# Cross-attention values per tile with their sums, divided behind the product, in a decoder layer

## The chip, the cores and the metric

One core of a Trainium2 chip runs the whole kernel in one launch. The metric is the device time of one execution, in microseconds (us), as the median of several. PE is TensorE, DVE VectorE, ACT ScalarE, POOL GpSimd, SP the sync engine that only launches DMAs here.

## What is computed

A decoder layer over 2 x 1024 tokens of 256 numbers, 16 heads of 16, float32: self-attention, then cross-attention over 77 context rows with a mask, then a mixture of 8 experts with the two best for each token; after each a residual and a layer norm. The part at issue, shortened:

```python
energy = jnp.einsum('bhqd,bhkd->bhqk', Q, K) * scale
energy = jnp.where(m == 0, -1000000000.0, energy)
attn = jax.nn.softmax(energy, axis=-1)
out = jnp.einsum('bhqk,bhkd->bhqd', attn, V)
out = out.transpose(0, 2, 1, 3).reshape(B, S, HID)
return out @ Wo + bo
```

## The kernel before

The stages are self-attention (to about 490 us), cross-attention (`for n in range(NT)`, 16 tiles of 128 tokens, n = 4g+i, `TG` = 4 groups), and the experts (46 blocks of 128 sorted rows).

Cross-attention of tile n before the change:
- PE `scores2(n)` (L611): scores of 16 heads into banks 0 to 3 (`quad`, columns 0 to 307), three tiles ahead of the values (`FAR = 3`).
- DVE `take(n)`: L1062 copies them out with the mask by a minimum (`s2_taken`), L1069 takes each head's maximum. POOL `shift(n)` subtracts it, ACT `exp2(n)` is the exponential, in place in `sc2`.
- DVE `sum_probs(n)` (L1074, L1076): sums over 77 and reciprocals. POOL `divide(n)` (L1798) multiplies them in; the last two tiles' on DVE (`last_divide`, L1092).
- PE `turn_probs(n)` (L629): ten 128-wide transposes in three pieces into banks 4 and 5, each piece copied to `pT` by ACT (L1516).
- PE `values2(g, half)` (L648): once for four tiles, with the placed values `vbd` as the stationary side and 512 queries moving; the result lies turned, [channel, query], in banks 6 and 7. ACT copies it to `o2T`, `project_o2(g)` (L657) multiplies by Wo, and DVE `residual2(g)` adds it to `xres` and takes moments; POOL `root`, DVE `root_moments` and `norm_x2(g)` (L1110) end the norm.

Between these lie, once for each group: `turn_x1` (L589) and `project_q2` (L596) for the next group's queries; `turn_x2` (L669) and `logits2` (L693) for the experts' router; DVE `top_two`. ACT `keep_high` writes the bf16 high half of the rows to send, `low_x2` (L1175, DVE) the low half. When half of the tokens are ranked (`rank(0)`, `rank(1)` on PE), DVE `place(0)` (L1141 to L1161) works out their sorted rows, `rowof`; POOL `scatter` (L1785) sends 8 tiles twice with indirect DMAs, SP waits for all 16 and loads the first blocks (L425), and PE `turn_block` (L843) begins the experts.

Of the kernel before, what the change touches and what calls it, by code (L numbers as in the profile page):

```python
# [5 lines left out]
ALU = mybir.AluOpType  # L6
# [7 lines left out]
P = 128  # L14
B, S, D = 2, 1024, 256
H, HD = 16, 16
SC = 77
# [16 lines left out]
SR = 4  # L34
FAR = 3
# [4 lines left out]
PAIR_CHUNKS = [(2 * j * SC // P, ((2 * j + 2) * SC - 1) // P) for j in range(HALF // 2)]  # L40

# [19 lines left out]
MASK_STEPS = 9  # L61
SOON = 14
LATE = 6
# [13 lines left out]
def build(nc, t):  # L77

    with ExitStack() as ctx:
# [65 lines left out]
        vbd = sb("vbd", [P, B, 2, VC, P])  # L145
# [60 lines left out]
        sum2 = sb2("sum2", [P, SR, H])  # L206
        inv2 = sb2("inv2", [P, SR, H])
        pT = sb2("pT", [P, 2, VC, 512])
        o2T = sb2("o2T", [P, 2, 512])
        logits = sb2("logits", [P, NT, NE])  # L210
# [30 lines left out]
        last_shifted, last_divided = sem("last_shifted"), sem("last_divided")  # L241
# [4 lines left out]
        s2_summed, s2_recip, p2_done, p2_turned, pT_done = map(sem, ("s2_summed", "s2_recip", "p2_done", "p2_turned", "pT_done"))  # L246
        o2_ready, o2T_done = sem("o2_ready"), sem("o2T_done")
# [36 lines left out]
        SCORED = (9, 13)  # L284
        X2_BANK = (6, 6, 0)
# [32 lines left out]
        def _(sp):  # L318
# [11 lines left out]
            def load_late():  # L330

                late = [(w_in[n][:, :, :], t[n].rearrange("(c p) n -> p c n", p=P)) for n in ("cwq", "cwo")]
                late += [(before[:, :], t["before"]), (b1[:, :, :], t["b1"].rearrange("e (c p) -> p e c", p=P)),
# [56 lines left out]
            for h, s0, n, c, row in V_RUNS:  # L390
                sp.dma_start(vbd[row:row + n, :, :, c, h * HD:(h + 1) * HD].rearrange("p b h d -> p (b h) d"),
                             v2[s0:s0 + n, :, :].rearrange("p b (h d) -> p (b h) d", h=2)[:, :, h * HD:(h + 1) * HD]).then_inc(v2_placed, 16)
# [47 lines left out]
            sp.wait_ge(o2_ready, 2 * TG)  # L440
# [18 lines left out]
        def _(pe):  # L459
# [139 lines left out]
            def scores2(n, half):  # L599

                g, i = n // 4, n % 4
                if half == 0:
# [4 lines left out]
                    if n == NT - 2:  # L607
                        pe.wait_ge(ranks_taken, 1)
# [27 lines left out]
            def values2(g, half, queries=slice(0, 4 * P)):  # L636

                if half == 0:
                    pe.wait_ge(pT_done, 12 * g + 3 * (queries.stop // P))
                    pe.wait_ge(q2_done, min(2 * g + 4, 2 * TG))  # L640
                    if g:
                        pe.wait_ge(y2_done, 4 * g)
                        pe.wait_ge(x2T_done, min(2 * g, 2 * TG - 4))
# [1255 lines left out]
```

## Time and profile before

| | us |
|---|---|
| median of 3 runs | 855.1 (852.06 to 857.89) |
| the profiled execution's own time | 856.25 |
| its span, first to last instruction | 854.4 |
| DVE busy | 639.0 (75%) |
| PE busy | 713.2 (83%) |
| ACT busy | 487.8 (57%) |
| POOL busy | 305.5 (36%) |

The busy shares are means over the whole program; the change touches the stretch from about 490 to 630 us, so the rows below are read there. A timeline row is start, length, engine, line, operation, output<-inputs, shapes, count, and in brackets how long the engine had waited and for what.

### The profile page before, as it was taken

The page shows a single profiled execution, that of the slowest core. Times are in us where ns is not written, and L with a number is a line of the kernel's source. Part 1 is how long each engine was busy: PE and PEld are TensorE (multiplying, and loading weights), DVE is VectorE, ACT ScalarE, POOL GpSimd, SP SyncE. Part 2 cuts the span into 40 slices and gives each one's busy share as a digit, 9 for nine tenths or more (in the row PEclk, how much of TensorE's full clock was granted, in tenths as well). Part 3 has the DMA queues.
Part 4 walks back from the last instruction along what each step waited for, and adds up shares of the span by engine and source line. Part 5 has one row for each costly group of instructions (what it writes and reads, how often), then busy time and mean ns, then how long its engine had stood idle before and what let it go on. Part 6 is the DMA issues. An engine that isn't in the chain of part 4 may idle for free.

```text
span 854.4 us, 14878 instructions
## 1 busy us (share of the span) xinstructions
PE 713.2 (83%) x4760; PEld 332.1 (39%) x4760; DVE 639.0 (75%) x1087; ACT 487.8 (57%) x982; POOL 305.5 (36%) x249
## 2 busy tenths in 40 slices
PE   6789999999999999999998868867679888789800
PEld 3442222223222222222222235545367566667600
DVE  3487888877888888887875689999737446689765
ACT  2225677777777677776777554342436566457622
POOL 8000600000000398881002575666712554444411
PEclk9898999999999999999999888887679999899965
DMA  7746040030400689883000090000241333412121
GB/s 196 187 110 148 16 93 21 19 75 20 94 20 25 155 239 278 260 253 125 2 1 1 1 380 14 1 2 7 75 124 52 100 105 90 143 53 90 58 99 49
DMA packets 51171, 80.75 MB, mean 95 GB/s; under 512 B 16468, under 2 KB 35415, under 8 KB 49689
## 3 DMA queue, kind: packets, MB, share of 16 engines
q1 hardware_dynamic: 37065, 44.91, 19.2%
q0 software_dynamic: 9952, 31.29, 11.8%
q10 hardware_dynamic: 4080, 3.61, 1.7%
q8 instruction: 42, 0.69, 0.4%
q14 instruction: 32, 0.26, 0.1%
HBM read 48.21 MB, written 33.11 MB: 95 GB/s over the span
## 4 chain that ended last, share of the span: by engine, by line
PE 54%; DVE 26%; DMA 6%; issue 5%; ACT 4%; POOL 2%; SPq 1%; DVEq 1%; another core or an unknown queue 1%; ACTq 0%; POOLq 0%
PE bank L544 12%; PE bank L536 12%; PE quad L517 11%; DVE rowmax L959 6%; PE quad L868 6%; PE bank L885 5%; DMA kstack<-k_parts 3%; PE bank L468 2%; DVE hl L1189 2%; DVE sc L1062 2%; ACT probs L1495 2%; DVE sum L1074 2%; DVE max L1069 2%; DMA qstack<-q_parts 1%; DVE attn_all L1175 1%
## 5 line engine op out<-in xcount | busy, mean ns | idle before, releaser
L959 DVE TENSOR_REDUCE rowmax<-quad 128x1 f32<-128x1024 f32 x256 | 303.0, 1218 | 77.1 <-PE quad L517 76.5
L1495 ACT ACTIVATE probs<-bank 128x512 f32<-128x512 f32 x512 | 284.3, 595 | 115.6 <-PE bank L536 112.8
L536 PE MATMUL bank<-qstack,kstack 98*128 98x512 bf16 x512 | 195.0, 389 | 12.9 <-ACT probs L1495 11.2
L517 PE MATMUL quad<-kstack,qstack 96*128 96x512 bf16 x512 | 178.4, 388 | 15.2 <-DVE rowmax L959 6.6
L868 PE MATMUL quad<-xbT,w 128*128 128x128 bf16 x1104 | 121.1, 224 | 25.6 <-DVE hl L1189 16.0
L544 PE MATMUL bank<-probs,v_all 128*32 128x512 f32 x1024 | 140.3, 617 | 0.0
L536 PEld LDWEIGHTS bank<-qstack,kstack 98*128 98x128 bf16 x512 | 49.0, 97 | 193.9 <-ACT probs L1495 163.2
L868 PEld LDWEIGHTS quad<-xbT,w 128*128 x1104 | 91.3, 100 | 58.5 <-issue 43.3
L1619 ACT ACTIVATE hid<-quad,b 128x128 f32<-128x128 f32 x184 | 52.6, 369 | 65.1 <-PE quad L868 49.5
L517 PEld LDWEIGHTS quad<-kstack,qstack 96*128 96x128 bf16 x512 | 48.6, 99 | 77.4 <-DVE rowmax L959 39.8
L1839 POOL DMA_INDIRECT y_tokens<-ysb,dest x46 | 47.7, 1038 | 84.1 <-DVE ysb L1203 75.3
L1737 POOL DMA_DIRECT2D w1raw<-in_w x8 | 6.5, 806 | 188.1 <-PE bank L468 188.1
L885 PE MATMUL bank<-w,hh 128*128 x184 | 71.8, 392 | 1.7 <-DVE hl L1189 1.7
L1189 DVE TENSOR_TENSOR hl<-hid,hh 128x512 bf16<-128x512 f32 x46 | 42.8, 930 | 26.1 <-ACT hh L1625 23.2
L1773 POOL TENSOR_TENSOR lnv<-lnv,power 128x4 f32<-128x4 f32 (+1 forms) x14 | 19.1, 1367 | 109.4 <-DVE lnv L1014 109.0
L885 PE MATMUL bank<-w,hl 128*128 x184 | 51.3, 279 | 0.0
L1793 POOL TENSOR_TENSOR sc<-sc,max 128x1232 f32<-128x1232 f32 x15 | 34.4, 2296 | 45.0 <-DVE max L1069 45.0
L1516 ACT ACTIVATE pT<-bank 128x512 f32<-128x512 f32 (+1 forms) x48 | 23.7, 524 | 41.4 <-PE bank L629 41.1
L629 PE MATMUL bank<-ident,sc 128*128 128x128 f32 (+1 forms) x160 | 30.7, 337 | 15.7 <-POOL sc L1798 6.6
L1785 POOL DMA_INDIRECT x_sorted<-attn_all,rowof x32 | 32.8, 1024 | 17.4 <-issue 5.5
L1200 DVE TENSOR_TENSOR ysb<-bank,b 128x256 f32<-128x256 f32 x46 | 19.4, 422 | 25.5 <-PE bank L885 15.0
L1798 POOL TENSOR_TENSOR sc<-sc,inv 128x1232 f32<-128x1232 f32 x14 | 31.4, 2251 | 12.6 <-DVE inv L1076 12.6
(184 smaller groups left out, 951.3 us busy)
## 6 DMA issues: line engine op xcount, KB each, us to landing
xb<-x_sorted SPq DMA_DIRECT2D x46, 129.0 KB
x_sorted<-blank POOLq DMA_DIRECT2D x6, 774.0 KB, 9.1
w1raw<-in_w POOLq DMA_DIRECT2D x8, 512.0 KB, 6.1
w2raw<-in_w POOLq DMA_DIRECT2D x8, 512.0 KB, 6.3
w_split<-w1two POOLq DMA_DIRECT2D x8, 512.0 KB, 5.7
w_split<-w2two POOLq DMA_DIRECT2D x8, 512.0 KB, 4.4
w<-w_split SPq DMA_DIRECT2D x16, 256.0 KB, 5.2
w<-w_split SPq DMA_DIRECT2D x4, 1024.0 KB, 11.8
```

The lines of the kernel that those rows point to most:

```text
L517: mm = pe.matmul(bank[2 * (p % 2) + e], q, kstack[slot][0:MAXROW, j, e * 512:e * 512 + 512], start=True, stop=True)
L536: mm = pe.matmul(bank[4 + i % 2], kstack[slot][0:KROWS, j, kt * P:kt * P + P], qstack[slot][0:KROWS, half, j, :], start=True, stop=True)
L544: pe.matmul(bank[6][32 * j:32 * j + VW, :], v_all[:, u // 2, kt, j, :], probs[:, i % PR, :], start=(kt == 0), stop=(kt == KT - 1), skip_gr ...
L868: mm = pe.matmul(bank[m % 3][:, fc * P:(fc + 1) * P], w1[half][c][fc][:, bass.ds(at, P)], xbT[:, m % 3, 2 * part + c, :], start=(k == 0), ...
L885: mm = pe.matmul(bank[Y_BANK[m % 2]][:, 0:n], a[:, m % 2, fc, :], w2[fc][:, bass.ds(at * (2 * D // P), n)], start=(step == 0), stop=(fc == ...
L959: dve.tensor_reduce(rowmax[:, k % 2, p:p + 1], quad[:, 2 * (p % 2):2 * (p % 2) + 2, :].rearrange("p a n -> p (a n)"), AX_X, ALU.max).then_ ...
L1189: dve.tensor_tensor(hl[:, m % 2, :, :], hid[:, m % 2, :, :], hh[:, m % 2, :, :], ALU.subtract).then_inc(hl_done, 1)
L1495: act.activation(probs[:, i % PR, :], bank[4 + i % 2], ACT.Exp, scale=INV4).then_inc(probs_ready, 1)
L1619: act.activation(hid[:, m % 2, fc, :], bank[m % 3][:, fc * P:(fc + 1) * P], ACT.Relu, bias=b1[:, bass.ds(e, 1), fc]).then_inc(hid_done, 1)
L1785: pool.indirect_dma_start(xs[h], bass.IndirectOffsetOnAxis(ap=rowof[:, j, n:n + 1], axis=0), xsend[:, n, :], None).then_inc(scattered[h], 16)
L1793: pool.tensor_tensor(sc, sc, over_heads(max2[:, n % SR, :]), ALU.subtract).then_inc(s2_shifted, 1)
L1839: pool.indirect_dma_start(ys[h], bass.IndirectOffsetOnAxis(ap=dest[:, m % XB:m % XB + 1], axis=0), ysb[:, m % YB, :], None, bounds_check=2 ...
```

## The change

The division moves behind the value product. `vbd` gets a column of ones for each head (17 columns for a head, `OW`), so the product brings the sum along. `values2(n)` now runs for each tile, with `pT` stationary and `vbd` moving; the result has the queries on the partitions and goes into columns 308 to 443 of banks 0 and 1, beside the scores. DVE `scale2(n)` takes the reciprocal of the sums and multiplies, into `o2n`. `turn_o2(g)` on PE transposes four tiles to banks 6 and 7, from where it goes on as before. `sum_probs`, `divide` and `last_divide` go. All 16 `low_x2` tiles move from DVE to POOL, eight of them inside the stage. `turn_x1`, `turn_x2`, `turn_probs`, `project_o2`, `top_two`, `rank(0)`, `rank(1)` and `place(0)` get other places, and several waits are added.

```diff
-                if n < NT - 2:
-                    pe.wait_ge(p2_done, n + 1)
-                else:
-                    pe.wait_ge(last_divided, n - NT + 3)
+                pe.wait_ge(p2_exp, n + 1)
...
+                    if n > FAR:
+                        pe.wait_ge(o2_scaled, n - FAR + (1 if i == 0 else 0))
...
+            def values2(n):
+
+                i, b = n % 4, n // 4 // 2
+                pe.wait_ge(pT_done, 3 * n + 3)
+                pe.wait_ge(s2_taken, n + FAR if i == 1 else min(n + FAR + 1, NT))
+                if n:
+                    pe.wait_ge(o2_scaled, n)
+                for half in range(2):
+                    for c in range(VC):
+                        lo, hi = (0, HALF) if c == 0 else V_HEADS[c]
+                        mm = pe.matmul(O2[half][:, lo * OW:hi * OW], pT[0:VROWS[c], half, c, n % PT * P:n % PT * P + P],
+                                       vbd[0:VROWS[c], b, half, c, lo * OW:hi * OW], start=(c == 0), stop=(c == VC - 1), skip_group_check=True)
+                mm.then_inc(o2_ready, 1)
+
+            def turn_o2(g, tiles=range(4)):
...
+                for half in range(2):
+                    for i in tiles:
+                        tr = pe.transpose(bank[6 + half][:, i * P:i * P + P], o2n[:, i, half * P:half * P + P], ident[:, :])
...
+                    turn_probs(n, lambda k: None)
+                    values2(n)
+                    turn_x1(g + 1)
+                    for half in range(2):
+                        project_q2(g + 1, half)
                     for half in range(2):
                         next_scores(half)
...
+            def scale2(n):
+
+                out = quad[:, 0:2, FREE - 12:FREE - 12 + HALF * OW].rearrange("p a (h d) -> p a h d", d=OW)
+                inv = inv2[:, n % 2, :].rearrange("p (a h) -> p a h", a=2)
+                dve.wait_ge(o2_ready, n + 1)
+                dve.reciprocal(inv, out[:, :, :, HD]).then_inc(o2_recip, 1)
+                dve.wait_ge(o2_recip, n + 1)
...
+                dve.tensor_tensor(o2n[:, n % 4, :].rearrange("p (a h d) -> p a h d", a=2, d=HD), out[:, :, :, 0:HD],
+                                  inv.rearrange("p a (h o) -> p a h o", o=1).to_broadcast([P, 2, HALF, HD]), ALU.mult).then_inc(o2_scaled, 1)
...
-                if n == NT - 5:
-                    place(0)
                 if n + FAR in SCORED:
                     top_two(SCORED.index(n + FAR))
...
+                if n == NT - 4:
+                    place(0)
```

The rows of order below are the instructions of one engine in queue order, with the line numbers of their own kernel (those after the change differ). First PE around tile 5 (i = 1), before, from `turn_x1` to `turn_x2`:

```order
L589 MATMUL bank<-ident,x 128x128 x8
L629 MATMUL bank<-ident,sc 128x128 x8
L596 MATMUL bank<-x1T,cwq 128x512 x4
L629 MATMUL bank<-ident,sc 104x128 x2
L611 MATMUL quad<-kbd,q2T 128x154 x8
L669 MATMUL bank<-ident,xres 128x128 x8
```

and after, from the second half of V(5) to the scores of tile 9, L614 x8 being those of tile 8 (turned probabilities are L629, scores L614, V L646):

```order
L646 MATMUL quad<-vbd,pT 128x136
L646 MATMUL quad<-vbd,pT 128x51
L646 MATMUL quad<-vbd,pT 128x34
L646 MATMUL quad<-vbd,pT 128x51
L646 MATMUL quad<-vbd,pT 128x34
L592 MATMUL bank<-ident,x 128x128 x8
L599 MATMUL bank<-x1T,cwq 128x512 x4
L614 MATMUL quad<-kbd,q2T 128x154 x8
L629 MATMUL bank<-ident,sc 128x128 x8
L614 MATMUL quad<-kbd,q2T 128x154 x4
L629 MATMUL bank<-ident,sc 104x128 x2
L614 MATMUL quad<-kbd,q2T 128x154 x4
```

V(5) now stands ahead of `turn_x1` and of the projection; the turns of tile 5, which stood between these two, now lie ahead of V(5) (the L629 rows here are tile 6's), and the scores of tile 8 come behind all of it.

DVE, before, from the take of tile 13 to the first copy of `place(0)` (L1141):

```order
L1062 TENSOR_TENSOR sc<-quad,cap 128x1232
L1069 TENSOR_REDUCE max<-sc 128x16
L1175 TENSOR_TENSOR attn_all<-xres,attn_all 128x256 x4
L1074 TENSOR_REDUCE sum<-sc 128x16
L1076 RECIPROCAL inv<-sum 128x16
L1074 TENSOR_REDUCE sum<-sc 128x16
L1076 RECIPROCAL inv<-sum 128x16
L1141 COPY ranked<-quad 128x72
```

and after, from the last take (tile 15) on; `scale2` is L1082 and L1086, the residual L1106:

```order
L1070 TENSOR_TENSOR sc<-quad,cap 128x1232
L1075 TENSOR_REDUCE max<-sc 128x16
L1097 TENSOR_TENSOR sc<-sc,max 128x1232
L1082 RECIPROCAL inv<-quad 128x16
L1086 TENSOR_TENSOR o2n<-quad,inv 128x256
L1106 TENSOR_TENSOR xres<-bank,xres 128x256 x2
L1109 BN_STATS stats<-xres 128x6
L1106 TENSOR_TENSOR xres<-bank,xres 128x256
L1109 BN_STATS stats<-xres 128x6
L1106 TENSOR_TENSOR xres<-bank,xres 128x256
L1109 BN_STATS stats<-xres 128x6 x2
```

Seven operations of moments follow, and then `place(0)` (L1146): it now stands behind the last take, its shift, `scale2(12)` and `residual2(2)`.

POOL, before, from the first scatters on (L1793 is a shift, L1773 a root, L1839 sends an expert's output):

```order
L1798 TENSOR_TENSOR sc<-sc,inv 128x1232 x2
L1785 DMA x_sorted<-attn_all,rowof 2944x258 x2
L1793 TENSOR_TENSOR sc<-sc,max 128x1232
L1785 DMA x_sorted<-attn_all,rowof 2944x258 x2
L1773 TENSOR_TENSOR lnv<-lnv,power 128x4
L1785 DMA x_sorted<-attn_all,rowof 2944x258 x12
```

and after (L1772 shift, L1757 bias, L1778 low half, L1752 root, L1764 scatter):

```order
L1772 TENSOR_TENSOR sc<-sc,max 128x1232
L1757 TENSOR_TENSOR xres<-x,cbo_row 128x256 x2
L1772 TENSOR_TENSOR sc<-sc,max 128x1232
L1778 TENSOR_TENSOR attn_all<-xres,attn_all 128x256 x4
L1752 TENSOR_TENSOR lnv<-lnv,power 128x4
L1764 DMA x_sorted<-attn_all,rowof 2944x258 x16
L1778 TENSOR_TENSOR attn_all<-xres,attn_all 128x256 x4
L1752 TENSOR_TENSOR lnv<-lnv,power 128x4
```

All 16 scatters now stand in one piece behind the last shift and root.

## Rows read from the trace of the kernel before

**Rows 1.** Table of stretches: length; busy (count) of PE, PEld, DVE, ACT, POOL; clock; DMA.

```profile
489.50:615.50 126.00, 94.03 (x657) 61.13 (x656) 117.34 (x213) 53.74 (x90) 82.58 (x52) 0.83 0.21 78
615.50:628.10 12.60, 8.33 (x59) 5.75 (x59) 0.00 (x0) 3.06 (x6) 4.92 (x6) 0.64 0.43 131
628.10:854.40 226.30, 158.32 (x1713) 121.05 (x1713) 148.03 (x441) 116.71 (x316) 85.38 (x75) 0.88 0.27 85
```

**Rows 2.** Chain of waits of the cross stage, shares by line.

```profile
by line: DVE sc L1062 11.2%; DVE sum L1074 10.8%; DVE max L1069 9.2%; DVE attn_all L1175 7.1%; PE bank L629 7.0%; DVE xres L1110 5.1%; PE quad L611 4.3%; PE bank L693 4.2%; POOL sc L1798 3.6%; issue 3.3%; DVE x L1054 3.3%; DVE xres L1101 3.
```

**Rows 3.** DVE's groups, 535.5 to 572.9: count, busy us, mean ns, idle before.

```profile
L1069 DVE TENSOR_REDUCE max<-sc 128x16 f32<-128x1232 f32 x4 | 5.7, 1436 | 0.1
L1062 DVE TENSOR_TENSOR sc<-quad,cap 128x1232 f32<-128x1232 f32 x4 | 5.7, 1421 | 0.4 <-PE quad L611 0.4
L1074 DVE TENSOR_REDUCE sum<-sc 128x16 f32<-128x1232 f32 x4 | 5.6, 1412 | 0.0
L1175 DVE TENSOR_TENSOR attn_all<-xres,attn_all 128x256 bf16<-128x256 f32 x4 | 4.5, 1196 | 0.0
```

**Rows 4.** Timeline, 592 to 629: start, us, engine, what.

```profile
592.01 1.92 DVE L1146 TENSOR_TENSOR fill<-upto,blocks 128x64 f32<-128x64 f32 x1
...
595.39 0.17 DVE L1155 CAST rowof<-rowf 128x16 uint32<-128x16 f32 x1
...
605.34 1.03 POOL L1785 DMA_INDIRECT x_sorted<-attn_all,rowof  x1 [0.19 <-issue]
...
620.99 0.96 POOL L1785 DMA_INDIRECT x_sorted<-attn_all,rowof  x1 [0.31 <-issue]
...
623.57 2.69 SPq L425 DMA_DIRECT2D xb<-x_sorted  x6
...
628.12 1.01 PE L843 MATMUL bank<-ident,xb 128*128 128x128 bf16 x8
```

**Rows 5.** Timeline of DVE and POOL around `norm_x1` and a sum.

```profile
516.45 1.38 DVE L1054 TENSOR_SCALAR x<-xres,lnv 128x256 f32<-128x256 f32 x4
...
550.36 1.42 DVE L1074 TENSOR_REDUCE sum<-sc 128x16 f32<-128x1232 f32 x1
...
551.99 3.23 DVE L1054 TENSOR_SCALAR x<-xres,lnv 128x256 f32<-128x256 f32 x4
...
552.15 2.27 POOL L1798 TENSOR_TENSOR sc<-sc,inv 128x1232 f32<-128x1232 f32 x1 [2.00 <-DVE inv L1076]
```

**Rows 6.** Three lines: duration ns min/median/max, first and last start.

```profile
L1225 DVE RECIPROCAL rden<-bank x16: 246/247/258, 99.4 to 489.7; 128x16 f32<-128x16 f32 x16
...
L1229 DVE TENSOR_TENSOR attn_all<-bank,rden x16: 423/424/425, 99.7 to 490.0; 128x256 f32<-128x256 f32 x16
...
L1778 POOL TENSOR_TENSOR xres<-x,cbo_row x16: 726/732/937, 456.2 to 586.5; 128x256 f32<-128x256 f32 x16
```

**Rows 7.** Timeline of PE: one half of the values, and router logits twice.

```profile
545.65 1.93 PE L648 MATMUL bank<-pT,vbd 128*32 128x512 f32 x16 [0.50 <-ACT pT L1516]
...
624.68 3.58 PE L693 MATMUL quad<-wg,wqkv 128*128 128x8 f32 x16 [3.80 <-ACT wqkv L1544]
...
650.15 1.85 PE L693 MATMUL quad<-wg,wqkv 128*128 128x8 f32 x16
```

**Rows 8.** Timeline of PE: turns of probabilities, of x1, scores, output projection.

```profile
489.54 1.04 PE L629 MATMUL bank<-ident,sc 128*128 128x128 f32 x8
...
491.82 1.09 PE L589 MATMUL bank<-ident,x 128*128 128x128 f32 x8
...
498.13 0.81 PE L611 MATMUL quad<-kbd,q2T 32*128 32x154 f32 x16 [0.56 <-ACT q2T L1530]
...
550.70 3.72 PE L657 MATMUL bank<-cwo,o2T 128*128 128x256 f32 x16 [0.32 <-ACT o2T L1537]
```

**Rows 9.** Stretches: length, PE busy (count), granted clock, DMA share, GB/s.

```profile
508.10:512.80 4.70, 4.20 (x18) 0.50 1.01 420
513.60:519.80 6.20, 5.96 (x44) 1.00 0.02 7
```

More of the change, by code:

```diff
@@ L34 @@
 SR = 4
+PT = 3
 FAR = 3
@@ L283, in build @@
         Y_BANK = (6, 7)
-        SCORED = (9, 13)
-        X2_BANK = (6, 6, 0)
+        SCORED = (10, 14)
+        X2_BANK = (6, 6, 2)
+        O2 = [quad[:, half, FREE - 12:FREE - 12 + HALF * OW] for half in range(2)]
         BLOCKS = 2 * HB
@@ L634, in turn_probs @@
                         logits2(SCORED.index(n + FAR))
[L636 to L643, printed above, removed]
-                        pe.wait_ge(logits_taken, min(g, 2))
-                for k in range(2):
-                    for j, chunks in enumerate(PAIR_CHUNKS):
-                        c, out_rows = chunks[k], slice(2 * HD * j, 2 * HD * j + 2 * HD)
-                        mm = pe.matmul(bank[6 + half][out_rows, queries], vbd[0:VROWS[c], g // 2, half, c, out_rows], pT[0:VROWS[c], half, c, queries],
-                                       start=(k == 0), stop=(k == 1), skip_group_check=True)
-                if queries.stop == 4 * P:
-                    mm.then_inc(o2_ready, 1)
+            def values2(n):
[10 more added lines that the diff above has]
+                mm.then_inc(o2_ready, 1)
@@ L1055, in norm_x1, with take @@
                                       ALU.subtract, ALU.mult).then_inc(x1_done, 1)
-            def take(n, between=None):
+            def take(n):
                 dve.wait_ge(s2_ready, n + 1)
@@ L1286, in _ @@
                 if i == 1:
-                    if 0 < g < TG - 1:
+                    scale2(n)
+                    if g:
+                        root_moments(4 * g - 4, 4 * g)
                         norm_x2(g - 1)
-                    sum_probs(n + 1)
-                    if g == TG - 1:
-                        last_divide(n + 1)
-                    sum_probs(n + 2)
-                    if g == TG - 1:
-                        last_divide(n + 2)
-                elif i == 3 and g < TG - 1 or i == 0 and 0 < g < TG - 1:
-                    sum_probs(n + 1)
-                    if n == NT - 5:
-                        sum_probs(n + 2)
+                if n + FAR < NT:
+                    take(n + FAR)
+                if n + FAR == NT - 1:
+                    last_shift()
+                if i != 1:
+                    scale2(n)
                 if i == 0 and g:
@@ L1321, in _ @@
                     start_moments(KT, NT)
-                if i == 2 and 0 < g < TG - 1:
-                    low_x2(g - 1)
-            root_moments(NT - 8, NT - 4)
-            norm_x2(TG - 2)
             top_two(TG - 2)
@@ L1591, in _ @@
                 keep_turned(n)
[L1592 to L1600 removed]
+                if n + FAR - 1 < NT and n < NT - 1:
+                    exp2(n + FAR - 1)
+                if i == 0 and g:
+                    keep_o2(g - 1)
+                if i == 1 and g < TG - 1:
+                    keep_x1T(g + 1)
+                    keep_q2(g + 1)
+                if i == 2 and g:
                     keep_x2(g - 1)
@@ L1830, in _ @@
                     root(2, KT, NT)
-            for k in range(2, HT):
+                if i == 3 and g:
+                    low_x2(g - 1)
+            for k in range(HT):
                 for j in range(2):
                     scatter(k, j)
+            low_x2(TG - 2)
             def send_block(m):
```

163 lines of the change are left out of this document (59 added, 104 removed).

## The prediction

> **What bounds the kernel now.** I read the table of stretches first [rows 1]. The cross-attention stage runs from 489.5 to 615.5 us of the trace; in it DVE is busy 117.3 of 126 us, PE 94.0, POOL 82.6, ACT 53.7. Then 12.6 us pass in which DVE does nothing, and at 628.1 the experts' stage starts. The chain of waits in the stage goes mostly over DVE [rows 2]: score minimum (L1062), sum (L1074), maximum (L1069), low halves (L1175). So DVE is the bound of this stage now; the gap behind it is set by something else. DVE's groups in one period of four tiles, 535.5 to 572.9 (37.4 us), are in [rows 3]; the sums are 5.6 us of them and the low halves 4.5.
>
> What starts the experts [rows 4]: `place(0)` ends with `rowof` at 595.39+0.17 = 595.56; POOL launches 16 scatters behind it, the last at 620.99+0.96 = 621.95, SP launches the sorted blocks from 623.57, and PE turns the first at 628.12, directly behind its router logits. Two chains end there together: the last tiles, and the scatters with the block loads.
>
> **What the change does to each engine's work.** DVE: a sum with its reciprocal takes 551.99-550.36 = 1.63 us in the stream [rows 5]. 14 of the 16 pairs lie in the stage: -22.8. Two `last_divide` of 1.44: -2.9. Eight low halves, in two groups of four at 4.5 like the one in [rows 3]: -9.1. Added: `scale2`, 16 times. The trace has the same pair of operations on the same shapes out of PSUM in `normalise` (0.25 and 0.42, starting 0.29 apart: 0.71) [rows 6], so +11.4. POOL loses 14 divides of 2.25 (-31.5) and gains 16 low halves. Nothing there shows a low half on POOL; the nearest is the bias add on the same shape, 0.73 [rows 6]. I take 0.7 each; POOL has room, and behind them in its queue stands only the next shift, which ACT needs two tiles later. So at up to 1 us each they cost nothing. The constants of ones are one small load on SP's queue and one POOL copy before the weights are split, where POOL had been idle: 0.
>
> The divides also held DVE: four `norm_x1` tiles took 1.38 us at 516.45, with POOL idle, and 3.23 at 551.99, with a divide beginning at 552.15; one of them then waited for it [rows 5]. With 1.9 us like this for two `norm_x2`, one `norm_x1` and the three-step root before tile 3, DVE would win 7.7 in all. The Trainium skill, page "GPSIMD Engine Reference", section "1. Specifications", says that GpSimd contends with VectorE for shared SBUF interfaces when that runs a 2-port mode or has two SBUF inputs; the two rows agree.
>
> PE: `values2` was 3.86 us per four tiles (1.93 for each half) [rows 7]. Now it is ten matmuls per tile, each with its own 128x128 fp32 load. Sixteen such with 8 columns took 1.85 us at full clock and 3.58 at half (650.15 and 624.68) [rows 7], 0.11 or 0.22 each; the two with 136 columns cost about what a transpose of 128 does, 0.13. V, my name for it, is then 1.3 us at full clock, 2.5 at half: 5.2 to 10 per four tiles. Eight turns of `o2n` add 1.05. PE's work per four tiles so grows by at least 2.4 us.
>
> **What decides: the handoff.** The value products now go into banks 0 and 1, where the scores lie. V(n) waits until DVE has read scores n+3, and S, the scores that come later, wait until DVE has read V. Where DVE formerly always had two or three tiles in store, PE and DVE now take turns. Queued behind PE's wait in V(n) are the next turns and scores; ACT waits for those turns, DVE for the scores. The Trainium skill, page "PSUM — Partial Sum Buffer", section "PSUM bank collisions raise a hardware error", says that TensorE may not write a bank while VectorE reads it, also at other columns; no row before the change tests it. By it these waits can't be loosened; without it V(n) would lose about 1.4 us of waiting per tile.
>
> I lay out the period from the end of S(8), the scores of tile 8, to that of S(12). A take is 1.44 us for L1062 and 1.44 for L1069 [rows 3]; project o2 is 3.7 [rows 8].
> - Take 8, then the minimum of tile 9: 0.07+2.88+1.44 = 4.4 us; V(6) 1.3.
> - Turn x2 1.1, half a turn of probabilities 0.5, ACT's copy 0.5, logits 1.85 to 2.7 (2.3), the rest of tile 7's turns and S(10) 2.0: 6.4.
> - Minimum of tile 10: 1.5; V(7) 1.35. Sum 14.95.
> - DVE alone: scale 0.75, norm_x1 1.4 (in one period only), top two 2.2 to 2.9 (2.5), minimum of tile 11 1.45. Sum 21.05. PE has been idle about 2.5 us by then.
> - V(8) 1.3 or 2.5 (1.9), project o2 3.7: 26.65.
> - T(9) to V(9): turn, two copies and a third, then V, 3.6 [rows 8]: 30.25.
> - Turn x1, ACT, project q2, ACT, S(12): 498.13+0.81-491.82 = 7.1 [rows 8]. 37.35.
>
> That is the same 37.4 us as now: the 10 us taken off DVE come back as idle time of DVE. Before, turns of probabilities and old scores filled the last two steps; now V stands ahead of them and S(12) behind both.
>
> **The sum.** First tiles: V(0) can start at 494.2, when scores 3 are read (492.77+1.42); +1.9+3.6+7.1: S(4) ends at 506.8, where it now ends at 498.9. From it 4.4, V(2) 1.3, scale 0.7, attention add 2.0, moments 1.0, minimum of tile 6 1.5, V(3) 2.5 at half clock behind a wait of 2.7, PE's turns and scores 5.2 (3.5 or 7.0), V(4) 1.3, and 3.7+3.6+7.1: S(8) ends at 541.1, now 532.7. One period: S(12) at 578.5. Tile 12, without norm_x1: 19.65 to the last minimum, 598.1; V(12) 1.9, project 3.7, residual 0.9, moments 0.9: 605.5. Only then stands `place(0)`: 4.74 us as now, 2.6 without the two operations that a divide held [rows 4]: rowof at 608.1. The scatters now run without a break: 16 of them at 1.27 (the pace of the last five) to 1.42 (the twelve launches from 605.34 to 620.99 [rows 4]) are 20.0 to 22.3, take 21.1, to 629.6; +1.6 to SP's launch: 631.2 against 623.57, +7.6. The first block had landed by 628.12 at the latest, and not before SP's six launches began; so PE starts 5.8 to 7.6 later, and I take 7. PE's own chain (tiles 13 to 15 at 3.6 to 5, x2, logits) ends near 623 and is covered by this. If the scatters were faster, it would count from about -5.
>
> The experts' stage is PE's (158 of 226 us busy against DVE's 148) [rows 1]; the eight low halves that leave DVE there stand under PE's work, so 0. It would cost at most 3 if POOL's four low halves held `send_block(1)`; six output buffers cover that.
>
> The profiled run took 856.25 us with its span of 854.4, 1.15 above the median 855.1. 856.25+7 = 863.3, as a median **862**.
>
> **The rivals.**
> - *DVE stays the bound, faster.* Then before `rowof` DVE loses twelve sums 19.6, low halves 9.1, held time 7.7, and gains 13 scales 9.3, the last take with its shift 4.4 and residual with moments 3.9: -18.8; scatters uninterrupted another -6. The tail of PE then starts the experts at about 604: 832 us. For it: DVE is 93% busy, PE 75%. Against: the turns above. It decides from the point where a period falls under 30 us. Chance 0.10.
> - *Partly hidden.* PE's full clock throughout and quick copies make periods of 34: 840 to 853. Chance 0.08.
> - *The clock.* Stretches after PE's idle times run at 0.50 for 3 to 5 us (508.10 to 512.80, behind 3.15 us idle) and then at 1.00 (513.60 to 519.80) [rows 9]; the stage's mean is 0.83. PE's part of a period is 23 us; if another third of it is at half, 7 us per period, 2.5 periods: +17, 879 us. Chance 0.07.
> - *The forecast,* with both ends of its unknowns: all at full clock, no held operations, block landed early: -8 from the sum, 854; V and the projections mostly at half, `place` held, slow scatters: +10, 872. Chance 0.75.
>
> Range 847 to 873: it leaves out the DVE case, a part of the partly hidden one, and the clock. One per cent, 8.6 us, is about what this kernel's measurement can tell from nothing. Slower by more: 0.34 of the forecast and 0.07: 0.41. Within: 0.41+0.04: 0.45. Faster: 0.10+0.04: 0.14.
>
> **What would show it.** The mean of V's matmuls; DVE idle of 20 us or more in the stage, released by PE's scores and value products; periods of about 37 us between scores of tiles 4k; `rowof` near 608 and the first block's launch near 631; PE idle some 10 us before the first block, released by its load. I am wrong if DVE stays over 90% busy, if `rowof` comes before 600, or if PE's tail and not the load starts the experts.

## The result, and the profile after

The changed kernel takes 897.9 us (median; 893.8 to 898.7) against 853.6 before: ratio 1.051, 95% interval 1.046 to 1.057. It is slower by 44 us, where 7 were forecast.

The table of stretches of the changed kernel, in the columns of [rows 1]: from the first turn of tile 0 to the first turned block, and the experts' stage.

```profile
483.89:665.68 181.79, 152.80 (x907) 125.94 (x906) 81.98 (x219) 58.32 (x99) 62.97 (x56) 0.71 0.17 61
665.68:891.97 226.29, 158.97 (x1713) 121.37 (x1711) 144.45 (x423) 116.10 (x314) 89.03 (x79) 0.88 0.28 87
```

The experts' stage has its old length of 226.3 us. The first stretch was 138.6 us before (489.54 to 628.12; PE 102.34 busy, DVE 117.34, clock 0.81) and is 181.8 now: +43.2. (This execution's self-attention ended 5.6 us earlier, so the two spans differ by 37.6.) DVE fell from 117 to 82 us, as meant. PE rose from 102 to 153, by 50, and its mean clock fell from 0.81 to 0.71. So PE is now the bound, and the question is what its 50 us are. The value products V(n) are 37.6 of them (57.9 against 20.3), the new turns of `o2n` (L660) 7.2, and the rest is other work of PE at the lower clock.

The groups of lines in that stretch: count, busy us, mean ns of one, idle before.

```profile
L646 PE MATMUL quad<-vbd,pT 128*128 128x51 f32 (+3 forms) x320 | 57.9, 356 | 15.7 <-issue 10.5 <-ACT pT L1496 3.6 <-DVE sc L1070 1.7
L646 PEld LDWEIGHTS quad<-vbd,pT 128*128 128x128 f32 (+1 forms) x320 | 56.2, 271 | 19.9 <-issue 14.4 <-ACT pT L1496 5.4
L629 PE MATMUL bank<-ident,sc 128*128 128x128 f32 (+1 forms) x160 | 31.7, 342 | 4.1 <-issue 2.9 <-ACT pT L1496 1.2
L660 PE MATMUL bank<-ident,o2n 128*128 128x128 f32 x32 | 7.2, 391 | 3.1 <-DVE o2n L1086 3.1
L1778 POOL TENSOR_TENSOR attn_all<-xres,attn_all 128x256 bf16<-128x256 f32 x12 | 7.7, 674 | 0.0
L1086 DVE TENSOR_TENSOR o2n<-quad,inv 128x256 f32<-128x256 f32 x16 | 6.8, 425 | 0.6
L1082 DVE RECIPROCAL inv<-quad 128x16 f32<-128x16 f32 x16 | 4.1, 256 | 53.8 <-PE quad L646 35.9 <-remote 17.8
```

The count is what to look at: the program issues 160 value products, ten per tile, and the trace has 320 records. Each float32 product leaves two records, each with a weight load of its own; a transposition in float32 leaves one (160 issued on L629, 160 recorded). The eight router matmuls behind [rows 7] left sixteen in the same way. DVE waits 35.9 us for the value products.

The chain of waits in the stretch is PE's now, where [rows 2] had DVE. V makes up 29.3% of it, V(0) and V(1) at 4.5 us each. The longest piece of all stands at the end, 17.8 us in which DVE's `scale2(15)` is held by something that the trace can't name; it runs beside V(14), V(15) and the scatters, and is taken up again below.

```profile
by line: PE quad L646 29.3%; PE bank L629 11.7%; another core or an unknown queue 9.8%; PE quad L614 8.6%; PE bank L599 7.8%; issue 7.6%; PE bank L668 6.9%; DVE sc L1070 3.2%; PE bank L660 3.0%; PE bank L705 3.0%; ACT pT L1496 2.7%; PE bank
487.89 4.51 PE quad L646 x20
495.13 4.53 PE quad L646 x20
646.15 17.82 another core or an unknown queue
```

The clock, in four stretches of the same table (PE's busy time is the second number):

```profile
487.90:499.40 11.50, 11.03 (x50) 10.38 (x51) 2.00 (x3) 2.60 (x4) 2.25 (x1) 0.50 0.99 358
525.00:535.00 10.00, 9.99 (x53) 8.70 (x54) 5.26 (x11) 3.09 (x5) 2.25 (x1) 0.50 0.00 0
541.10:552.70 11.60, 9.30 (x64) 6.12 (x62) 4.99 (x21) 5.05 (x8) 1.01 (x1) 1.00 0.00 0
567.90:578.50 10.60, 10.40 (x54) 8.73 (x55) 7.18 (x28) 3.45 (x6) 4.81 (x5) 0.50 0.00 0
```

From 525 to 535 PE is recorded busy 9.99 of 10 us and is granted 0.50. The stretches at 0.50 hold V(n) with turns of probabilities; the one at 1.00 holds V(5) with `project_q2` and its 512 columns. Not every V is at half clock: nine of the 16 take 4.4 to 4.5 us, the other seven 2.41 to 2.65.

The chain of [rows 4] comes 45 us later in the trace, `rowof` 156.8 us into the stretch where it was 105.9:

```profile
640.71 0.17 DVE L1160 CAST rowof<-rowf 128x16 uint32<-128x16 f32 x1
641.19 1.10 POOL L1764 DMA_INDIRECT x_sorted<-attn_all,rowof  x1 [1.76 <-DVE rowof L1160]
...
660.38 0.96 POOL L1764 DMA_INDIRECT x_sorted<-attn_all,rowof  x1 [0.30 <-issue]
662.96 2.69 SPq L428 DMA_DIRECT2D xb<-x_sorted  x6
...
665.68 0.63 PE L851 MATMUL bank<-ident,xb 128*128 128x128 bf16 x4
```

From `rowof` to the first turned block 25.0 us pass, where 32.7 passed before: the scatters in one piece win back 7.8 of the 51. PE doesn't wait for the load here; it waits 3.1 us for `scale2(15)`, and turns the block 2.7 us after the launch. In the runs v5, v2, v5wide and v2late below it does wait for the load, and turns the block 2.1 us after the launch. So the tail of PE costs about 0.6 us here (an estimate from these two times), and the load sets the rest.

### The profile page after: what moved, and what is told of

Same layout as the page of the kernel before. It is cut to its first block, busy times and chain, and to the rows that moved or that the text cites. A ratio compares the mean times of both kernels' runs of the same rounds, so it can differ in the third digit from the quotient of the medians.

```text
span 892.0 us, 15293 instructions
## 1 busy us (share of the span) xinstructions
PE 758.9 (85%) x4952; PEld 390.1 (44%) x4952; DVE 595.5 (67%) x1069; ACT 488.4 (55%) x982; POOL 282.8 (32%) x252
## 4 chain that ended last, share of the span: by engine, by line
PE 65%; DVE 15%; DMA 6%; issue 5%; ACT 4%; another core or an unknown queue 2%; SPq 1%; POOL 1%; DVEq 1%; ACTq 0%; POOLq 0%
PE bank L547 11%; PE bank L539 11%; PE quad L520 10%; PE quad L646 6%; PE quad L876 5%; DVE rowmax L967 5%; PE bank L893 5%; PE bank L471 2%; DMA kstack<-k_parts 2%; PE bank L629 2%; DVE hl L1188 2%; PE quad L614 2%; PE bank L668 2%; ACT probs L1476 2%
## 5 line engine op out<-in xcount | busy, mean ns | idle before, releaser
L1476 ACT ACTIVATE probs<-bank 128x512 f32<-128x512 f32 x512 | 284.0, 595 | 110.8 <-PE bank L539 108.0
L876 PE MATMUL quad<-xbT,w 128*128 128x128 bf16 x1104 | 121.7, 224 | 24.8 <-DVE hl L1188 16.1
L547 PE MATMUL bank<-probs,v_all 128*32 128x512 f32 x1024 | 137.5, 605 | 0.0
L876 PEld LDWEIGHTS quad<-xbT,w 128*128 x1104 | 91.4, 100 | 57.9 <-issue 42.5
L1598 ACT ACTIVATE hid<-quad,b 128x128 f32<-128x128 f32 x184 | 52.6, 368 | 66.4 <-PE quad L876 53.8
L646 PE MATMUL quad<-vbd,pT 128*128 128x51 f32 (+3 forms) x320 | 57.9, 356 | 15.7 <-issue 10.5
L1772 POOL TENSOR_TENSOR sc<-sc,max 128x1232 f32<-128x1232 f32 x15 | 33.8, 2254 | 102.6 <-DVE max L1075 102.6
L646 PEld LDWEIGHTS quad<-vbd,pT 128*128 128x128 f32 (+1 forms) x320 | 56.2, 271 | 19.9 <-issue 14.4
L1752 POOL TENSOR_TENSOR lnv<-lnv,power 128x4 f32<-128x4 f32 (+1 forms) x14 | 19.5, 1395 | 129.7 <-DVE lnv L1022 129.7
L1070 DVE TENSOR_TENSOR sc<-quad,cap 128x1232 f32<-128x1232 f32 x16 | 23.1, 1441 | 48.5 <-PE quad L614 48.4
L1082 DVE RECIPROCAL inv<-quad 128x16 f32<-128x16 f32 x16 | 4.1, 256 | 53.8 <-PE quad L646 35.9
```

Source lines behind the costliest of these rows:

```text
L547: pe.matmul(bank[6][32 * j:32 * j + VW, :], v_all[:, u // 2, kt, j, :], probs[:, i % PR, :], start=(kt == 0), stop=(kt == KT - 1), skip_gr ...
L646: mm = pe.matmul(O2[half][:, lo * OW:hi * OW], pT[0:VROWS[c], half, c, n % PT * P:n % PT * P + P], vbd[0:VROWS[c], b, half, c, lo * OW:hi ...
L876: mm = pe.matmul(bank[m % 3][:, fc * P:(fc + 1) * P], w1[half][c][fc][:, bass.ds(at, P)], xbT[:, m % 3, 2 * part + c, :], start=(k == 0), ...
L1476: act.activation(probs[:, i % PR, :], bank[4 + i % 2], ACT.Exp, scale=INV4).then_inc(probs_ready, 1)
L1598: act.activation(hid[:, m % 2, fc, :], bank[m % 3][:, fc * P:(fc + 1) * P], ACT.Relu, bias=b1[:, bass.ds(e, 1), fc]).then_inc(hid_done, 1)
L1772: pool.tensor_tensor(sc, sc, over_heads(max2[:, n % SR, :]), ALU.subtract).then_inc(s2_shifted, 1)
```

## The experiments

Three theories. **A**: V's price, ten float32 matmuls with their loads per tile. **B**: the handoff, V waiting for the take and the scores for V's scaling. **C**: the clock. A fourth, **D**, is the place of `place(0)` and the scatters. Four of the kernels (v5, v2, v5wide, v2late) leave out value products, and with them a part of the output; they only price the rest. Stage below is the stretch from the first turn of tile 0 to the first turned block; each length is from the one profiled run of a kernel, each ratio from all runs, against the kernel before on the same chip.

**Half of V's matmuls (v5).** In `values2` and the constants:

```diff
-                    for c in range(VC):
+                    for c in (0, 1, VC - 1) if half == 0 else (0, VC - 1):
...
-        "vone": np.stack([...
+        "vone": np.ones((P, VC * HALF), np.float32),
```

> The changed kernel with five of the ten value matmuls of each tile (chunks 0, 1 and the last of the first half, 0 and the last of the second) and the constant of ones all ones; the other value products are left out of the output. Everything else, every wait and its place, stays. In the changed kernel's trace the value matmuls take 57.9 us of PE between the start of the stage and the first turned block, 20 records for each tile. Theory A, the price of the value matmuls is what moved the time: half of it goes, 29 us, V(n) is 1.25 us at full clock and 2.3 at half, about what the forecast had put in, and the time falls to 865 to 872 us. Theory B, the handoff through banks 0 and 1 and the new order cost it, however short V is: each period keeps its waits for the take and the scaling, the time falls by under 12 us and stays over 886. Theory C, V's small matmuls also hold the clock at half: with half of them gone the stage's mean clock rises from 0.71 to above 0.80 and the other PE work of the stage (96 us) shrinks too, 855 to 862.

Measured: 873.7 us, 1.023 (1.019 to 1.027); stage 159.4 us at clock 0.73. Half of V gives back 24 us: A's direction and near its size, at the slow end (865 to 872 expected). The clock hardly rose, so C in that form (above 0.80) is out.

**A fifth of V's matmuls (v2).** As v5 with `for c in (0,)`, and the accumulation ended there.

> The changed kernel with two of the ten value matmuls of each tile (chunk 0 of each half) and the constant of ones all ones; the rest of the value products is left out of the output. V(n) is then 0.5 us at full clock. Theory A: the value matmuls fall from 57.9 to about 12 us; if PE stayed the bound all the way, the time would be 898-46 = 852; if DVE or the handoff takes over below some length of V, the step from five matmuls to two gives less than the 17 us that it takes off PE, say 5 to 12, 855 to 864. Theory B: over 880, little below the run with five. What is left above the 853.6 of the kernel before is the floor that the handoff and the order set; the forecast's own period with V at 0.5 would be 33 us instead of 37.35, three periods and the last tiles shorter by about 15 in all, 847.

Measured: 863.3 us, 1.011 (1.008 to 1.015); stage 149.3, clock 0.75, PE busy 106.5. As A had it with a floor: five matmuls fewer gave 24 us, three fewer again gave 10.

**The same matmuls, all columns (wide).**

```diff
-                        lo, hi = (0, HALF) if c == 0 else V_HEADS[c]
+                        lo, hi = 0, HALF
```

> The changed kernel with each of the ten value matmuls over all 136 columns of its half instead of the 17 to 51 that hold something (the added products are zeros). Its output is the same. Theory A with the weight load as the price (in the changed kernel's trace the loads of these matmuls take 271 ns each on average, the matmul records 356 at its mean clock): V stays 2.45 us at full clock and 4.5 at half, and the time is that of the changed kernel within 4 us, 894 to 902. If the columns are the price, V doubles at least and the time passes 940. Theory C, the clock falls because these matmuls stream few columns: with 136 columns the stage's clock rises above the 0.71 of the changed kernel, and if V doesn't get longer, the time falls by 10 to 25 us.

Measured: 877.1 us, 1.030 (1.026 to 1.033). With more columns and the same output it is 18 us faster (2.1%, the intervals are apart). Its stage in the table of stretches:

```profile
486.16:648.60 162.44, 124.75 (x907) 103.69 (x906) 82.72 (x219) 57.31 (x99) 63.28 (x56) 0.89 0.19 68
```

One V(n) of it in the timeline, part of it at full clock and part at half:

```profile
547.70 4.23 PE L646 MATMUL quad<-vbd,pT 128*128 128x136 f32 x20 [1.61 <-issue]
```

The clock is 0.89 instead of 0.71 and the stage 19.4 us shorter. At full clock V(n) takes 2.56 to 2.59 us here and 2.41 to 2.44 in the changed kernel (V(5), V(9), V(12), V(13)): the columns cost some 0.15 us per tile. The rest is a price per matmul. The trace has weight loads beside 2.32 of the 2.44 us of V(13), which makes the load the likely price; no run takes it away. So C is right in this form: with V's matmuls on all columns the granted clock is higher, and the time goes with it. By what rule the chip grants it, these rows don't tell.

**Five matmuls of all columns (v5wide).** Both edits together.

> The kernel of run wide (all 136 columns of a half in each value matmul) with five of the ten value matmuls of each tile, ones constant all ones; the other value products are left out. It prices V apart from the clock. Run wide took 877.1 us, V(n) 2.56 us there at full clock and 4.87 at half, and run v5 873.7. Theory A (V's own time on PE): half of V goes in each of 16 tiles, 26 us of PE work, of which the stage with the handoff gives back at least 14: 858 to 864 us. Theory C (the clock alone, V's length doesn't matter once the clock is up): 874 to 877. If the handoff holds the rest, v5wide ends at v5's 873.7 less the clock's part, 865 to 870.

Measured: 868.5 us, 1.015 (1.011 to 1.019); stage 149.2, clock 0.83. Against wide, half of V is 1.45% or 12.4 us: V's own time matters with the clock mended too, between the two estimates, where the third (865 to 870) had it. Against v5 it shows C a second time: the same five matmuls on all columns, clock 0.83 instead of 0.73, the stage 10.2 us shorter (149.2 against 159.4), the time 0.8% or 7 us, with intervals that just touch. This run is also a test of the forecast's layout, since V now costs nearly what it had put in (29.3 us in 16 tiles, 1.8 us each):

| from the first turn of tile 0, us | forecast | v5wide | wide | changed kernel |
|---|---|---|---|---|
| S(4) ends | 17.3 | 17.2 | 18.1 | 26.5 |
| S(8) ends | 51.6 | 52.6 | 57.0 | 68.9 |
| S(12) ends | 89.0 | 93.0 | 101.2 | 116.0 |
| rowof | 118.6 | 124.7 | 137.4 | 156.8 |
| first block turned | 145.6 | 149.2 | 162.4 | 181.8 |

(The forecast's times less 489.5.) The layout of the handoff holds to 1 us up to tile 8, to 4 at tile 12 and to 6 at rowof.

**An idle matmul in the gap before V (after_fill).**

```diff
                 pe.wait_ge(pT_done, 3 * n + 3)
+                for _ in range(1):
+                    pe.matmul(bank[4 + (n + 1) % 2], ident[:, :], w_in["cwq"][:, :, :].rearrange("p c n -> p (c n)"), start=True, stop=True)
                 pe.wait_ge(s2_taken, n + FAR if i == 1 else min(n + FAR + 1, NT))
```

> The changed kernel with one idle matmul more per tile, of 128x512 in float32 on constants, whose product nothing reads: it stands between the scores of tile n+3 and V(n), where PE waits 1.61 us for DVE's take (nine such waits in the changed kernel's trace). A matmul of this shape takes 0.93 us at full clock (3.70 us for the four of project_q2 in run wide) and 1.9 at half. V keeps its narrow columns. Theory C (the clock falls in the stretches in which PE streams the narrow V and idles beside it, and that is worth about 20 us): with the gap filled the stage's mean clock rises from 0.71 to 0.80 or more and the time falls by 5 to 20 us from 897.9, to 878 to 893, though PE has 16 matmuls more. Rival (the clock is a matter of V's own columns, or wide gained by something else): the clock stays near 0.71, the matmuls at half clock overrun the gap by 0.3 us each, the ones without a gap cost 1.9, and the time is 900 to 915.

Measured: 892.0 us, 1.041 (1.033 to 1.049). The stage in the table of stretches:

```profile
489.12:664.29 175.17, 140.76 (x938) 106.59 (x937) 84.91 (x213) 57.58 (x99) 63.58 (x56) 0.87 0.19 70
```

Its groups of lines on PE (L641 is the added matmul, L648 the narrow V):

```profile
L648 PE MATMUL quad<-vbd,pT 128*128 128x51 f32 (+3 forms) x320 | 43.8, 298 | 7.7 <-DVE sc L1072 7.7
L629 PE MATMUL bank<-ident,sc 128*128 128x128 f32 (+1 forms) x160 | 25.8, 293 | 10.1 <-issue 8.6 <-ACT pT L1498 1.5
L641 PE MATMUL bank<-cwq,ident 128*128 128x512 f32 x32 | 19.6, 697 | 8.5 <-ACT pT L1498 8.5
```

The clock rises to 0.87. The same narrow products take 43.8 us instead of 57.9, the turns 25.8 instead of 31.7, and the stage is 6.6 us shorter though PE has 19.6 us of matmuls more that nothing needs. C is shown by an edit that doesn't touch V. In time it is 1% and the intervals touch (1.046 to 1.057 without it), but the stage hides most of it. Up to `rowof`, the changed kernel and this one:

```profile
483.89:640.71 156.82, 135.77 (x816) 110.20 (x815) 76.24 (x188) 52.67 (x86) 44.85 (x36) 0.72 0.14 54
489.12:630.14 141.02, 122.14 (x837) 90.68 (x835) 79.43 (x189) 51.94 (x86) 45.41 (x36) 0.92 0.16 60
```

`rowof` comes 15.8 us earlier (19.4 in wide). Behind it 34.2 us pass instead of 25.0: ACT's copies for the last tiles stand beside the scatters and are held 16.7 us in all by what the trace calls remote, and the block is turned 11.7 us after the launch. (Of the waits of 1.61 us before V, put at nine in the expectation, the changed kernel's trace has six.)

**V one place later (wide_late).** Run wide with V(n) of tiles 2, 3, 6, 7, 10, 11 behind the next tile's first turn, and those of 1, 5, 9 behind `turn_x1`:

```diff
                     tr.then_inc(p2_turned, 1)
+                    if j == 0 and n - 1 in LATE_V:
+                        values2(n - 1)
...
                     turn_probs(n, lambda k: None)
+                    turn_x1(g + 1)
                     values2(n)
-                    turn_x1(g + 1)
```

`scale2` moves with V on DVE, and the scores that come behind a late V go in one piece behind the last turn.

> The kernel of run wide with six of the sixteen V(n) one place later (tiles 2, 3, 6, 7, 10, 11: behind the first turn of the next tile instead of directly behind the scores whose take they wait for), V of the tiles 1, 5 and 9 between turn_x1 and project_q2, and DVE's scale2 moved with them. The computation is the same. In run wide PE waits 1.61 us before each of those V(n) and 0.74 between turn_x1 and project_q2. Theory B (the take that V waits for is what PE loses): 6 times 1.6 less about 0.5 that the scores then wait for scale2, and 3 times 0.7, in all 7 to 10 us: 867 to 870 us. If PE's waits are only moved to where the scores wait for scale2: within 2 us of 877. If the tail (V(15), the last logits, the stalls beside the scatters) sets the end and not the tiles: as little as 0 to 3.

Measured: 875.5 us, 1.023 (1.019 to 1.028) against wide's 1.030: 0.6%, about 5 us, less than B's 7 to 10, with intervals that overlap a little. Stage 158.1 instead of 162.4. PE's waits ahead of V fell from 15.3 to 3.5 us (those that the trace calls issue), and its scores now wait 10.2 us for `scale2`, where they hadn't: most of the wait was moved.

**The same with a fifth of V (v2late).** Run v2 in that order.

> The kernel of run v2 (two of ten value matmuls, the rest of the value products left out) with the order of run wide_late. Run v2 took 863.3 us, and its stage up to the first turned block 149.3 us against 138.6 in the kernel before, though V is only 0.5 us: this excess belongs to the handoff and the order. If PE's wait for the take in front of V makes it up, 6 times 1.1 to 1.6 and 3 times 0.7 us come back: 853 to 857 us. If it is the chain at a group's end (turn, copy, turn_x1, copy, project, copy, scores) and the place of place(0): 860 or more.

Measured: 870.7 us, 1.018 (1.015 to 1.021), slower than v2 by 0.7%: a miss. PE is busy less (100.9 us against 106.5), yet the stage is 154.8 us against 149.3. B's account, in which the take before V is what PE loses, doesn't carry over. PE's waits show where the gain went: ahead of V they fell from 16.1 to 3.2 us, and four scores now wait 17.8 us for `scale2`, which v2 doesn't show at all.

```profile
PE quad L646 <- issue: 16.1, 9, 3.1
PE quad L615 <- DVE o2n L1093: 17.8, 4, 5.7
```

(The first line is v2's, the second v2late's: total, times, longest.)

**The ranks first (wide_late_place).** Run wide_late with the ranks ahead of V(12) on PE and, on DVE:

```diff
                 if n + FAR == NT - 1:
                     last_shift()
+                    place(0)
...
-                if n == NT - 4:
-                    place(0)
```

> Run wide_late (1.0234 of before) with the ranks ahead of V(12) and project_o2 on PE and place(0) directly behind the last shift on DVE, so that rowof and the sixteen scatters no longer wait for V(12), project_o2(2), residual2(2) and its moments. The computation is the same. Theory D (the scatters' chain starts the experts): rowof comes 6 to 8 us earlier; the last tiles end about with the scatters in run wide_late, so of it only 1 to 4 us reach the time: 1.019 to 1.022. If the tail of the tiles, delayed by place's 2.6 us on DVE, sets the start: 0 to 3 us slower than wide_late.

Measured: 878.6 us, 1.028 (1.023 to 1.032). `rowof` comes 6.0 us earlier in the stage (126.5 against 132.5), and the first block is turned 5.6 us later (163.7 against 158.1). That doesn't refute D, because the scatters didn't come earlier: in POOL's queue a root stands ahead of them, which waits for the moments of `residual2(2)`.

```profile
622.97 1.02 POOL L1760 TENSOR_TENSOR lnv<-lnv,power 128x4 f32<-128x4 f32 x1 [14.48 <-DVE lnv L1029]
624.18 1.10 POOL L1772 DMA_INDIRECT x_sorted<-attn_all,rowof  x1 [0.19 <-issue]
```

The first scatter starts 133.1 us into the stage, in wide_late 133.0, and the loads are launched at 154.8 in both. What comes later is the tail of PE: between V(13) and V(15) its chain stands 16.2 us behind ACT copies that are held beside the scatters, where wide_late has 4.7. So an early `rowof` wasn't tested down to the load. What the other traces say for D is that `rowof` and the first block keep their distance, 24.3 to 25.6 us in the changed kernel, v5, v2, wide, v5wide, wide_late, v2late and wide_lowdve; after_fill and this run, with the held copies, are the exceptions.

**The low halves alone (lowpool).** The kernel before with only `low_x2` moved to POOL:

```diff
-                if i == 2 and 0 < g < TG - 1:
-                    low_x2(g - 1)
...
+                if i == 2 and 0 < g < TG - 1:
+                    low_x2(g - 1)
```

(The first is in DVE's program, the second in POOL's, behind the shift.)

> The kernel before with one part of the change alone: the low halves go from DVE to POOL, those of tiles 0 to 7 behind the shift of the third tile of a group, those of 8 to 11 behind the scatters, the last four ahead of send_block(1). The values stay as they were, probabilities first divided. In the kernel before DVE is busy 117.3 of the 126 us from 489.5 to 615.5, and two groups of four low halves lie there, 9.1 us. If DVE is the bound of that stage, as the forecast said: the stage is 5 to 9 us shorter, 845 to 849 us. If POOL's operations (0.67 us each in the changed kernel) hold DVE in its shared port or delay POOL's own divides, of which ACT and PE wait: within 3 us of before, or up to 5 slower. The eight low halves of the experts' stage: no effect, that is PE's.

Measured: 851.9 us, 0.999 (0.997 to 1.001). No gain: DVE's busy time fell by 6.5 us (117.3 to 110.8), the stage by 0.9 (137.7). So "DVE is the bound", as the forecast read [rows 1, 2], is too simple: with 6.5 us less to do, DVE waits for the others instead: 4.8 us for ACT's exponentials (2.2 before), 2.2 for POOL's bias adds (none before) and 2.0 for scores (0.6). The wait for the bias adds stands near where the halves had stood:

```profile
550.70 2.03 DVE L1054 TENSOR_SCALAR x<-xres,lnv 128x256 f32<-128x256 f32 x3 [2.19 <-POOL xres L1766]
```

**The low halves back on DVE (wide_lowdve).** Run wide with `low_x2` on DVE, in groups of four.

> The kernel of run wide with the low halves back on DVE (those of tiles 0 to 7 in the stage, in groups of four, the last eight among the experts' blocks, as the kernel before has them). In the changed kernel's stage DVE is busy 83 of 182 us. My theory: DVE has room, the 9 us hide, and the time is run wide's 877.1 within 3 us. Rival: POOL's low halves are in the way (they stand before the next shift, of which ACT waits) or DVE's are: more than 4 us in either direction.

Measured: 886.4 us, 1.036 (1.032 to 1.039): 0.6% slower than wide, where I had expected nothing. The group of four is short here, and its cost is not its length:

```profile
569.26 1.43 DVE L1180 TENSOR_TENSOR attn_all<-xres,attn_all 128x256 bf16<-128x256 f32 x4
570.60 0.19 DVE L1122 TENSOR_TENSOR logits<-bank,bg 128x32 f32<-128x32 f32 x1
...
570.94 1.06 PE L660 MATMUL bank<-ident,o2n 128*128 128x128 f32 x8 [0.91 <-DVE logits L1122]
```

It stands ahead of the add of the logits, for which PE's turn of `o2n` waits 0.91 us at this place. Twice 1.4 us don't make 5, and 1.5 to 1.7 us of the difference stand already at S(4) and S(8), before the first group runs (S(8) ends 58.5 us into the stage against 57.0, the group starts at 81.1). The intervals overlap a little. So at most some 4 us can be the halves' doing, and how they do it is open.

**The idle matmul in the kernel before (before_fill, low_fill).** In `turn_probs`, ahead of the wait for the divide; low_fill is lowpool with it.

```diff
+                if n:
+                    pe.wait_ge(pT_done, 3 * n - 1)
+                    for _ in range(1):
+                        pe.matmul(bank[4 + n % 2], ident[:, :], w_in["cwq"][:, :, :].rearrange("p c n -> p (c n)"), start=True, stop=True)
                 if n < NT - 2:
                     pe.wait_ge(p2_done, n + 1)
```

> The kernel before with one such idle matmul (128x512, float32, product unread) ahead of each tile's turns of probabilities but the first, where PE waits for POOL's divide (6.6 us in all) and for the copies. In the kernel before the clock of the stage is 0.81 and about 45 of its 139 us are granted at 0.50. Theory C with PE's clock mattering there too: clock over 0.88, time down by 3 to 10 us. Theory that DVE bounds that stage and the clock costs it nothing: within 3 us of before. Rival: the matmuls delay the turns, 3 to 12 us slower.

> Run lowpool (low halves on POOL, time unchanged at 0.999 of before) with the same idle matmul. Taking 9 us off DVE gave nothing there; if that is because PE at its reduced clock was as late as DVE, then both together give what neither does alone, 5 to 12 us faster than before (843 to 850). If DVE, POOL and ACT hold each other in a ring in which PE's clock has no part: within 3 us of before, as lowpool.

Measured: 854.3 us, 1.001 (0.999 to 1.004), and 853.3 us, 0.998 (0.995 to 1.001). The stage of before_fill:

```profile
484.67:623.73 139.06, 106.80 (x745) 66.98 (x743) 120.55 (x215) 56.79 (x96) 87.75 (x57) 0.90 0.23 83
```

The clock rises from 0.81 to 0.90 and the stage stays at 139.1 us. In the kernel before PE's clock costs nothing; in the changed one it costs about 18 us by run wide. None of these kernels beats the one before.

## Why the prediction was wrong

**The step that failed** is the price of V: "Sixteen such with 8 columns took 1.85 us at full clock and 3.58 at half", "0.11 or 0.22 each", hence V 1.3 us at full clock and 2.5 at half. The sixteen were records of eight matmuls; a matmul with its own float32 load costs twice that. V measured 2.41 to 2.44 us at full clock and 4.4 to 4.5 at half, 3.6 on average. Divided by its 20 records that is 0.12 or 0.22, so the price per record was right and the count was wrong. The forecast's own rows held the hint: the eight scores of a tile (L611 x8 in the rows of order) stand as x16 in [rows 8]. The Trainium skill, page "FP8 and Floating Point Precision", section "TensorE Precision Notes", says that true FP32 is four passes through the array. The trace shows two records for each product, and tells nothing of passes within one.

**The same term once more, through the clock.** The forecast took V at a mean of its two prices and gave the falling clock 0.07, as a consequence of idle time ("Stretches after PE's idle times run at 0.50 for 3 to 5 us"). The kernel before had longer ones (0.50 from 603 to 619), and in the changed one the clock was 0.50 in stretches in which PE was busy 99.9%. Run wide, with the same matmuls on more columns, has 0.89 instead of 0.71 and is 18 us faster. The Trainium skill, page "TensorE: Matmul & The Clock Gate", section "What's actually happening", says that the clock follows how busy PE has been; the busy time of the profile's rows doesn't show that here.

**The 44 us in parts**, by the ratios: from the changed kernel to wide 2.1% or 18 us, the clock; from wide to v5wide 1.45% or 12 us, the half of V that the forecast hadn't counted; from v5wide to before 1.5% or 13 us, against 7 to 8 that the forecast had for a V of this size. The first two parts depend on the order. By v5 instead, half of V is 24 us and the clock 7: a longer V costs more at a low clock. Together they are 31 us either way. The other 5 to 6 us over the forecast lie mostly between S(8) and rowof in the table above, and which wait they are isn't shown.

Point by point:
- **The handoff cancels DVE's gain**: right in what came of it, though by lowpool DVE's time had been worth little to begin with; what was cancelled and what was never there to gain isn't parted. DVE is idle for PE's products, 36.2 us for scores and 35.9 for V, where 20 or more were forecast, and the layout holds in v5wide to 6 us at rowof. Its periods were 37.35 forecast, 40.4 in v5wide, 44.2 in wide, 47.2 in the changed kernel (S(8) to S(12)). In the changed kernel S(4) to S(8) took 42.3 and the way to S(4) 26.5, where 34.3 and 17.3 stood. Whether V could start while DVE still reads its bank wasn't tried.
- **place 2.6 us, sixteen scatters in 20.0 to 22.3, launch 1.6 behind them**: 2.6, 20.2 and 1.6, so the gain from scatters in one piece was forecast rightly. (The forecast's 608.1 and 21.1 make 629.2 and not 629.6; 0.3 us lie between `rowof` and the first scatter.) The first block was turned 2.7 us after the launch instead of 4: the forecast took that from a place where PE's logits had ended last.
- **scale2 0.71, low halves on POOL 0.7 at no cost**: 0.26 and 0.42, and 0.67. Right.
- **Held operations win 7.7**: `norm_x2` and `norm_x1` fell from 726 and 637 ns on average to 408 and 470, 5.2 us together; the attention adds fell by 1.0 more. Near the 7.7.
- **Low halves take 9.1 us off DVE**: the size was right, the worth wrong: DVE's busy time was no price of the stage (lowpool). And the 4.55 us of a group aren't its own length. POOL ran a shift and two bias adds beside it:

```profile
545.89 4.55 DVE L1175 TENSOR_TENSOR attn_all<-xres,attn_all 128x256 bf16<-128x256 f32 x4
546.05 2.36 POOL L1793 TENSOR_TENSOR sc<-sc,max 128x1232 f32<-128x1232 f32 x1 [3.90 <-DVE max L1069]
548.37 1.78 POOL L1778 TENSOR_TENSOR xres<-x,cbo_row 128x256 f32<-128x256 f32 x2
```

  With POOL idle beside it (wide_lowdve) a group takes 1.43.
- **DVE stays the bound (0.10)**: wrong in every run of the changed kernel; DVE is 45% busy there, and 61% with the shortest V (v2).
- **The load, not PE's tail, starts the experts**: within 0.6 us, though not as foretold. PE's last wait is 3.1 us for `scale2(15)` and not 10 for the load; in v5wide, with V near the forecast's length, it is 6.3 us for the load. In after_fill and wide_late_place the tail ends last.

## What to carry to other kernels

Before a price is taken per instruction from a grouped row, count how many the program issues there: here one float32 product is two records, each with a load, and one transposition is one. Making the wide operand the stationary one turned 16 long products for four tiles (3.9 us) into 40 short ones with a load each, 2.4 us for ten at full clock. When PE becomes the bound, look at the granted clock of stretches in which it is busy: V's narrow matmuls on all columns cost 0.15 us more per tile and gave back 18 us, while a higher clock in a kernel in which PE isn't the bound (before_fill) gave nothing. And when a step is moved ahead in one queue, look at what stands before its follower in the next queue (the root before the scatters in wide_late_place).

## What the hardware showed that was not expected

- A stretch of 10 us with PE busy 9.99 us at a granted clock of 0.50, and a stage at 0.87 on average instead of 0.71 once one matmul of 512 columns stood before each V.
- Four low halves on DVE took 4.55 us beside POOL's shift and bias adds and 1.43 us with POOL idle: a factor of three on the same shape.
- Beside the scatters DVE's `scale2(15)` sits 17.8 us behind something that the trace calls remote, although the last V had ended 5.7 us before it began; in wide it is 17.8 us again. In both it ends 1.0 to 1.1 us after the first blocks are launched. In after_fill and wide_late_place it is ACT's copies that are held, 16 to 17 us in all. What holds them isn't shown.
